# Encoder stage of a graph network: TensorE adds the own rows to the neighbour sums inside its turning products, in place of an addition on GpSimd

## The reference, cut to what matters

```
h = jnp.maximum(_layernorm(x, axis=-1), 0.0)
# gcn_conv, with self-loops; dis = 1/sqrt(degree by target)
norm = dis[row] * dis[col]
agg  = segment_sum(xw[row] * norm[:, None], col)        # own row and neighbours
z = relu(agg(x @ W_enc1) + b_enc1)
z = relu(agg(z @ W_enc2) + b_enc2)
z = relu(z @ W_dec1 + b_dec1);  x_hat = z @ W_dec2 + b_dec2
```

## Time and profile before

| | us |
|---|---|
| runs (three) | 8628.08, 8637.53, 8635.45 |
| median | 8635.45 |
| the profiled execution, its device time | 8638.8 |
| the profiled execution, its span | 8637.1 |
| encoder stage, from the first load issued to the last y | 4686.4 to 5524.0 |

### The profile page before, as it was taken

One profiled execution on the slowest core, in us unless ns is written; L12 is line 12 of the kernel. 1 busy time (PEld: TensorE's weight loads), 2 busy tenths in 40 slices (PEclk: granted clock), 3 DMA queues, 4 the chain that ended last, 5 costly groups with the idle time before them and its releaser, 6 DMA issues. The chain is left out here.

```text
span 8637.1 us, 110883 instructions
## 1 busy us (share of the span) xinstructions
PE 3652.6 (42%) x20396; PEld 2793.2 (32%) x20396; DVE 5444.9 (63%) x22718; ACT 2663.1 (31%) x6456; POOL 5223.9 (60%) x4583
## 2 busy tenths in 40 slices
PE   7103555555669999800001776400005863333100
PEld 1002333334658888700000555300004652222100
DVE  8766555557998999755556999511115666666654
ACT  0671000005663333222222666300002334444322
POOL 0005888884437777777775222477775457777577
PEclk9556566667889999955555888655557985555555
DMA  8894333337983333333335888400006973333343
GB/s 229 316 358 118 41 41 41 41 41 206 274 249 88 94 93 95 87 95 94 95 93 152 291 287 287 136 22 22 21 22 196 306 238 104 104 104 104 101 139 119
DMA packets 1050252, 1197.22 MB, mean 139 GB/s; under 512 B 205970, under 2 KB 868830, under 8 KB 1039671
## 3 DMA queue, kind: packets, MB, share of 16 engines
q1 hardware_dynamic: 861252, 937.39, 34.3%
q0 software_dynamic: 188928, 259.09, 13.7%
HBM read 642.13 MB, written 581.54 MB: 142 GB/s over the span
## 5 line engine op out<-in xcount | busy, mean ns | idle before, releaser
L665 ACT ACTIVATE dense<-dense,nbi,sc 128x128 f32<-128x128 f32 x2370 | 936.5, 482 | 239.6 <-DVE nbi L1203 168.0
L536 POOL DMA_INDIRECT dense<-t_xs,gidx x784 | 778.7, 993 | 266.5 <-issue 235.4
L406 POOL DMA_INDIRECT g<-t_src,gidx x398 | 398.1, 1000 | 774.1 <-DVE keyr L440 653.1
L1519 PE MATMUL ps<-w,dense 128*128 128x128 f32 x6272 | 807.7, 282 | 0.0
L552 DVE TENSOR_SCALAR sidx<-keyend 128x2 int32 (+1 forms) x784 | 138.0, 176 | 985.8 <-DMA dense<-t_y,gidx 805.0
L1519 PEld LDWEIGHTS ps<-w,dense 128*128 128x128 f32 x6272 | 732.8, 192 | 47.6 <-issue 0.4
L424 POOL DMA_INDIRECT t_acc<-tot,sidx x392 | 638.5, 1629 | 146.5 <-issue 129.9
L570 PE MATMUL ps<-tot,share 128*128 128x128 f32 x4 | 1.5, 487 | 1532.2 <-DVE tot L559 1532.2
L938 POOL TENSOR_TENSOR dense<-dense 128x1280 f32<-128x1280 f32 (+1 forms) x79 | 229.1, 2900 | 596.4 <-ACT dense L665 596.4
L1249 DVE SCALAR_TENSOR_TENSOR dense<-xT 128x256 f32<-128x256 f32 x1568 | 545.5, 418 | 30.3 <-ACT xT L1673 21.5
L483 PE MATMUL ps<-ident,keyr 128*128 128x128 f32 x394 | 118.5, 399 | 1047.8 <-DVE seq L453 600.3
(11 more groups left out here) (261 smaller groups left out, 12570.3 us busy)
## 6 DMA issues: line engine op xcount, KB each, us to landing
dense<-t_xs SPq DMA_DIRECT2D x78, 1320.0 KB, 6.3
dense<-in_x SPq DMA_DIRECT2D x156, 640.0 KB, 5.5
t_xs<-dense SPq DMA_DIRECT2D x98, 528.0 KB, 7.4
t_xs<-hb SPq DMA_DIRECT2D x78, 660.0 KB, 5.0
t_sum<-dense SPq DMA_DIRECT2D x98, 512.0 KB, 3.5
t_src<-dense SPq DMA_DIRECT2D x78, 640.0 KB, 4.0
t_acc<-dense SPq DMA_DIRECT2D x78, 640.0 KB, 5.2
dense<-t_acc SPq DMA_DIRECT2D x78, 640.0 KB, 5.9
```

The lines of the kernel that those rows point to most:

```text
L406: gp.indirect_dma_start(rows[:, p.k, c, :], None, table, bass.IndirectOffsetOnAxis(ap=gidx[:, p.k, c:c + 1], axis=0)) \
L536: gp.indirect_dma_start(rows[:, p.k, c, :], None, table, bass.IndirectOffsetOnAxis(ap=gidx[:, p.k, c:c + 1], axis=0)) \
L665: i = nc.scalar.activation(out_t[0:p, k, 0:D], in_t[0:p, k, :], ACT.Relu, bias=bias[0:p, k:k + 1], scale=scale[0:p, k:k + 1])
L1519: i = nc.tensor.matmul(ps[:, o:o + P], xm[:, p.w, k, c * P:(c + 1) * P], w1[:, k, :], start=False, stop=(k == R - 1))
```

## The change

POOL's `enc_add` is taken out, and with it the semaphore "add". PE now makes the sum while it turns: for each of the ten pieces, in place of one transpose of `ain2`, two ordinary products with the identity go into one accumulator, the first with the piece of `ain2`, the second with the piece of `h2`. Since the own rows no longer pass through DVE's multiplication by dis (`enc_scale`), ACT's scale has to hold dis twice, so DVE makes rs * dis * dis in two steps. DVE's `enc_scale` waits for the load of the sums, and SP's `enc_load` waits for "tr" of block b-3, since `h2` is now read by PE.

```
@@ phase L2
-        L2 = phase("node", NB + 1, LN + "nb join h add dz scal tr trc mm relu mm2 y",
+        L2 = phase("node", NB + 1, LN + "nb join h sc2 dz scal tr trc mm relu mm2 y",
@@ enc_load (SP)
                 if needed(b - SLOTS + 1):
-                    sp.wait_ge(L2["add"].sem, L2["add"].after(b - SLOTS + 1))
+                    sp.wait_ge(L2["tr"].sem, L2["tr"].after(b - SLOTS + 1))
@@ POOL
-            def enc_add(r, u, p):
-                b = r * SLOTS + u
-                gp.wait_ge(L2["h"].sem, L2["h"].after(b + 1))
-                gp.wait_ge(L2["lda"][u].sem, L2["lda"][u].after(r * 16 + 16))
-                gp.tensor_tensor(ain2[u][0:p], ain2[u][0:p], h2[u][0:p], ALU.add).then_inc(L2["add"].sem, 1)
-            node_loop(gp, (enc_add, 0))
@@ enc_h_scales (DVE)
                 nc.vector.tensor_tensor(sc[0:p, u, :], rs[0:p, :], dsl[0:p, u, :], ALU.mult).then_inc(L2["sc"].sem, 1)
                 v.wait_ge(L2["sc"].sem, L2["sc"].after(b + 1))
+                nc.vector.tensor_tensor(sc[0:p, u, :], sc[0:p, u, :], dsl[0:p, u, :], ALU.mult).then_inc(L2["sc2"].sem, 1)
+                v.wait_ge(L2["sc2"].sem, L2["sc2"].after(b + 1))
@@ enc_scale (DVE)
-                v.wait_ge(L2["add"].sem, L2["add"].after(b + 1))
+                v.wait_ge(L2["lda"][u].sem, L2["lda"][u].after(r * 16 + 16))
@@ enc_turn (PE)
                 pe.wait_ge(L2["scal"].sem, L2["scal"].after(b + 1))
+                pe.wait_ge(L2["h"].sem, L2["h"].after(b + 1))
                 if needed(b):
                     pe.wait_ge(L2["trc"].sem, L2["trc"].after(b))
                 for k in range(K):
-                    i = nc.tensor.transpose(ps[:, k * P:k * P + p], ain2[u][0:p, k, :], ident[0:p, 0:p])
+                    nc.tensor.matmul(ps[:, k * P:k * P + p], ain2[u][0:p, k, :], ident[0:p, 0:p], start=True, stop=False)
+                    i = nc.tensor.matmul(ps[:, k * P:k * P + p], h2[u][0:p, k, :], ident[0:p, 0:p], start=False, stop=True)
                 i.then_inc(L2["tr"].sem, 1)
```

## The result

The changed kernel takes 9364.11 us in the median (four runs, 9358.23 to 9372.04) against 8636.49 us for the kernel before on the same chip. The ratio is 1.0842, with a 95% interval of 1.0823 to 1.0861: it is slower by 8.4%, 728 us. The prediction was 9302 us, range 9175 to 9475.

The account below looks back on a forecast made before the run. DVE was taken to bound the kernel before; after the change, a 19.0 us loop (7.0 + 0.1 + 5.7 + 4.64 + 1.53) replaces 10.32 a block: +660 over 76 blocks, -4 + 11 at the ends, 9302 us, range 9175 to 9475.

Parts of the forecast that it names:

- What bounds the kernel before: Encoder stage: DVE sets the pace, 10.32 us a block; POOL's addition stalls its dsl copy about 2.4 us a block.
- The moved wait: SP's load of block b+1 waits until block b-2 is turned, closing a loop of 19.0 us a block.
- turn: PE's twenty products per block: 4.94 us at high clock plus 2.0 for a low-clock start, 7.0 us (6.2 to 7.8).
- hand-over PE to SP: From the turn's end to SP's load: 0.1 us, as between ACT's copy and the turn.
- load issued to join: From the load's issue to DVE's join: 5.7 us, from the stage's first load into an idle queue.
- join to variance: From DVE's join begun to variance done, with no POOL in the way: 4.64 us.
- variance to next turn: From variance done to turn begun, with ACT's copy and DVE's scale side by side: 1.53 us.
- Another time than 5.7 us: Sign of being wrong: in the changed kernel's profile the load would land in a time other than 5.7 us.
- The ends: Encoder stage's start and end: about 4 us gained before block 0's turn, about 11 us lost after block 76's.
- never through a whole one: Rival: PE's clock stays low through the whole turn, 9.22 us, 21.2 us a block, 9470 us; chance 0.09.
- The products have two records each: Against the rival of single-pass identity products on PE, about 3 us a turn, 15.0 us a block, 8998 us; chance 0.04.
- The faster case: Rival: DVE freed and load in time, PE bound at 9.6 us, DMA engines needing 9.0; 8589 us; chance 0.03.

Follow-up runs that it names:

- e3: Kernel before without POOL's addition, own rows left out of the sums, load waiting for h of block b-3; 8506.1 us, ratio 0.983.
- e6: e1 plus one unused POOL addition of constant tiles per block, started by h, which no other engine waits for; 8665.7 us, ratio 1.0020.
- e8: e1 with the load's wait put back from h to the turn, own rows still in their own buffer; 9377.0 us, ratio 1.0844.
- e1: Changed kernel with own rows in a buffer of their own and the load waiting for h, not the turn; 8541.9 us, ratio 0.988.
- e2: Kernel before with one line changed: the load waits until block b-3 is turned, not added; 9098.6 us, ratio 1.052.
- e4: Changed kernel with the turn again ten transposes of the sums, own rows left out, waits kept; 9004.9 us, ratio 1.041.
- e5: Changed kernel with 26 unread identity products per block on PE between its first and second product; 9380.4 us, ratio 1.0848.
- e9: Changed kernel with 35 unread identity products per block on PE; 10293.9 us, ratio 1.062, in a set where the kernel before took 9687.8 us.

## Why the prediction was right, and where its terms were off

**What bounds the kernel before: right.** POOL's addition stopped DVE for 2.4 us a block. Shown twice, by e3 (away, and the copy takes 0.17 us) and by e6 (put beside, and it takes 2.3).

**The moved wait: right, and it is the cause.** e8 and e1 differ in this wait alone and lie 835 us apart; e2 has it alone and is slower by 5.2%. The reading that found it was of three numbers in one block: when SP wants to load, when the new releaser is done, and how much slack the load has.

**The loop's terms.** From 38 blocks of the changed kernel between 4800 and 5600 us:

| term | predicted | measured | least to most |
|---|---|---|---|
| turn | 7.0 | 7.10 | 6.07 to 7.68 |
| hand-over PE to SP | 0.1 | 0.29 | 0.26 to 0.35 |
| load issued to join | 5.71 | 6.06 | 5.67 to 6.92 |
| join to variance | 4.64 | 4.76 | 4.75 to 4.92 |
| variance to next turn | 1.53 | 1.65 | 1.61 to 1.69 |
| sum | 19.0 | 19.86 | |

From the turn of block 0 (4702.87) to that of block 76 (6203.13) it is 1500.3 us, 19.74 a block. The missing 0.74 us, 76 times, are 56 of the 62 us by which the forecast was short. The mis-sized steps are these:

- *Load, 0.35 us, the largest.* The prediction took the stage's very first load, 5.71 us, over the median landing of 6.2, with the argument that the queue would be idle. The queue is idle (the DMA share from 5320 to 5322, before the load of 5321.44, is 0.00 in the window shown below), and the load takes 6.06 all the same; why is not shown. The median of 79 was the better row than a single case with a reason. It is no accident of one run: e2, e4, e5 and e8 all have 6.04 to 6.10. "Another time than 5.7 us" was one of the prediction's own signs of being wrong, and for this term it came.
- *Hand-over, 0.19.* Priced by a hand-over between ACT and PE. SP's queue, in its loop, takes 0.29 from the turn's end to the DMA's issue in every kernel in which it waits there.
- *Join to variance and on to the turn, 0.12 each.* Priced at the stage's start and in one block, where the small steps follow without the gap that the loop has.

**The turn: right by two errors that cancel, so its closeness is partly luck.** The record at the high clock was priced at 0.1235 us from a group of 20, which contains the run-out of the last one. In the long groups it is 0.11, start to start; 40 records take 4.7 us, not 4.94 (e9's least). And the clock rises later than was assumed, 4.9 us after the turn's start in the mean and not 4.4; the bounds, 2.8 to 6.2 us for 2.8 to 6.1, were right. The 7.10 leave 2.4 us of loss, not 2.0. Windows around the turn of 5315.10, columns as in the earlier trace rows:

```profile
5316.00:5317.50 1.50, 1.50 (x9) 1.50 (x9) 0.82 (x1) 1.50 (x5) 0.00 (x0) 0.50 0.00 0
5320.00:5322.00 2.00, 2.00 (x14) 1.52 (x13) 0.00 (x0) 0.00 (x0) 0.00 (x0) 1.00 0.00 0
```

Its records start 0.21 us apart, and 0.11 apart from about 5318.0, an early rise: with 6.07 us it is the shortest turn of the table.

**The ends.** The start gave back 4.3 us (first load to first turn 23.5 us for 27.8), as predicted. The end cost 15.5 in place of 11. Together 716 - 4 + 15.5 = 727.5 us, which is the measured difference.

**The rivals.** From block 2 on the clock was low at the start of each of the 75 turns that had a pause before them, but never through a whole one; the last two had no pause, and one of these ran at the high clock throughout. The products have two records each, 3160 records for 79 blocks. The faster case did not come, but its mechanism was real: with the slot free early the same change is faster, and by 107 us (8648.5 less 8541.9) rather than by the 46 forecast for it, since both of the floors that it used, PE's 9.6 and the DMA engines' 9.0, were too high (at most 8.7 and at most 8.6).

## What to carry to other kernels

When a step takes over the last read of a buffer, the load that refills the buffer waits for it: look at when the load is issued, how much slack it has, and in which round the new reader comes. If the new release lies behind a step that itself needs that load one round later, all terms of the way round add up, however idle the engines are, and what is saved in one of them comes off the pace (here 4.7 us off the turn took 4.6 off the pace). The remedy is cheap, either a buffer of its own for the operand or one round less of lag: here 1.2% and 1.0% faster than before, with the same products on PE that came with 8.4% more time. The gain is not PE's, though: leaving POOL's addition out and doing nothing in its place gives 1.7% (e3).

## What was not expected of the hardware

- DVE's copy of ten numbers per partition stood still until a POOL addition had ended, even one that reads two constants and that nobody waits for: 2.67 us for 0.17 (e6). BATCH_NORM_STATS beside such an addition did not (0.28 us, e2).
- With pauses of 2.0 to 3.7 us on PE the clock was at 0.50 in some or all of the turn that followed, in 71 of 73 cases (e5); with pauses of 0.2 to 1.4 us in 4 of 72 (e9). The clock was bought back with useless work at a gain of 2.1 us a block.
- The DMA engines carried 338 to 342 GB/s over 500 us of this stage at a share of 1.01 to 1.02 (e1, e3), where the kernel before had 281 at 0.87: the share of 0.87 multiplied by the pace of 10.32 gave 9.0 us, which was no floor, as 8.6 was reached.
